# Attention scores from two float32r parts in 64-row groups, in place of three bfloat16 parts in 72 rows

## What is computed

```python
q = split_heads(x @ Wq.T)          # 16 heads of 8, 4 sequences
k = split_heads(x @ Wk.T)
v = split_heads(x @ Wv.T)
q = _rope(q, pos); k = _rope(k, pos)
score = jnp.einsum('bqd,bkd->bqk', q, k)
score = jnp.where(causal[None], score, -jnp.inf)
attn = jax.nn.softmax(score / jnp.sqrt(jnp.float32(D_K)), axis=-1)
out = jnp.einsum('bqk,bkd->bqd', attn, v)
```

## Time and profile before

| what | us |
|---|---|
| median of 3 executions | 916.42 (909.37 to 917.06) |
| span of the profiled execution, first to last instruction | 855.6 |
| from the first tile of attention to the start of the second feed-forward layer | 202.3 to 717.9 |
| one steady stage of attention | 30.31 |

### The profile page before, as it was taken

How to read it: one execution, slowest core, us unless ns; L and a number is a source line. 1 busy time by engine, 2 the same in 40 slices (tenths; PEclk the granted TensorE clock), 3 DMA queues, 4 the chain that set the end, 5 groups by cost and what they waited for, 6 DMA issues and landing times. The chain is left out here.

```text
span 855.6 us, 17846 instructions
## 1 busy us (share of the span) xinstructions
PE 779.7 (91%) x5570; PEld 427.9 (50%) x5570; DVE 610.9 (71%) x1919; ACT 507.4 (59%) x1229; POOL 315.4 (37%) x603
## 2 busy tenths in 40 slices
PE   9889999887899999999999999999999997689995
PEld 8888896543233333333333333333333335579884
DVE  4657774698668777788878878788787722856663
ACT  2166651673247767667667766766777684146662
POOL 6177742475104223223322422331242231056753
PEclk8699999998569999999999999999999998789998
DMA  8721113065332033033113303312320001122110
GB/s 271 270 57 50 54 33 117 23 169 159 57 57 45 14 57 57 10 49 58 34 26 57 53 6 57 58 22 36 57 41 18 3 1 34 73 70 50 52 42 26
DMA packets 27989, 51.84 MB, mean 61 GB/s; under 512 B 7552, under 2 KB 19200, under 8 KB 26496
## 3 DMA queue, kind: packets, MB, share of 16 engines
q1 hardware_dynamic: 21296, 41.04, 20.7%
q0 software_dynamic: 4096, 8.69, 3.8%
q10 hardware_dynamic: 2512, 1.06, 0.5%
HBM read 35.40 MB, written 14.97 MB: 59 GB/s over the span
## 5 line engine op out<-in xcount | busy, mean ns | idle before, releaser
L1448 DVE CUSTOM_DVE_ANT_0 cst<-psS,mask_row 128x768 bf16<-128x768 f32 (+7 forms) x512 | 364.7, 756 | 100.2 <-PE psS L1308 97.6
L1412 ACT ACTIVATE prob<-psST 128x512 f32<-128x512 f32 (+3 forms) x750 | 317.3, 495 | 158.9 <-PE psST L1339 155.2
L1353 PE MATMUL a_psO<-prob,vs 128*32 128x512 f32 (+3 forms) x1536 | 166.7, 506 | 2.8 <-ACT prob L1412 1.7
L1532 POOL TENSOR_TENSOR a_gate<-a_zeros 1x1 f32<-1x1 f32 x128 | 23.7, 185 | 333.7 <-ACT prob L1412 333.7
L1339 PE MATMUL psST<-a_qs,ks 75*128 75x512 bf16 (+1 forms) x480 | 123.7, 327 | 5.9 <-ACT prob L1412 3.5
L1308 PE MATMUL psS<-ks,a_qs 72*128 72x512 bf16 (+2 forms) x480 | 119.0, 337 | 5.6 <-DVE a_rowmax L1448 5.5
L777 POOL DMA_INDIRECT tok<-rows,f_there_number x64 | 61.8, 966 | 86.0 <-DVE f_number L489 42.0
L1308 PEld LDWEIGHTS psS<-ks,a_qs 72*128 72x128 bf16 x480 | 35.6, 99 | 101.1 <-DVE a_rowmax L1448 33.0
L1308 PE MATMUL psS<-ks,qs 72*128 72x512 bf16 (+3 forms) x288 | 75.8, 354 | 6.7 <-DVE a_rowmax L1448 6.5
L1533 POOL TENSOR_SCALAR_AFFINE_SELECT prob<-prob 128x512 f32<-128x512 f32 x128 | 80.3, 627 | 0.0
L1339 PE MATMUL psST<-qs,ks 75*128 75x512 bf16 (+3 forms) x270 | 73.4, 346 | 2.7 <-ACT prob L1412 1.7
(11 more groups left out here) (183 smaller groups left out, 1066.1 us busy)
## 6 DMA issues: line engine op xcount, KB each, us to landing
a_qs<-q_split SPq DMA_DIRECT2D x60, 96.0 KB
rows<-tok SPq DMA_DIRECT2D x8, 536.0 KB, 4.9
ks<-k_split SPq DMA_DIRECT2D x32, 128.0 KB
qs<-q_split SPq DMA_DIRECT2D x36, 96.0 KB
q_split<-p_part SPq DMA_DIRECT2D x24, 128.0 KB, 2.4
k_split<-p_part SPq DMA_DIRECT2D x24, 128.0 KB, 2.4
ks<-k_split SPq DMA_DIRECT2D x16, 192.0 KB
tok<-x_after_first SPq DMA_DIRECT2D x4, 536.0 KB, 5.4
```

Source lines behind the costliest of these rows:

```text
L1353: last = nc.tensor.matmul(psO[32 * h:32 * h + 32, c0:c0 + w], vs[r][:, j, h, :], prob[:, u % RING, h, 0:w], start=(j == 0), stop=(u + 1 in ...
L1412: nc.scalar.activation(prob[:, u % RING, h, 0:w], score_buffer(s, u * QH + h)[:, 0:w], ACT.Exp, scale=SCALE).then_inc(exp_done, 1)
L1448: last = nc.vector.tensor_tensor_reduce(out=out[:, a * CH:a * CH + width], in0=ps[:, a * CH:a * CH + width], in1=mask_row[:, S - width:], ...
```

## The change

q and k are rounded into two float32r parts of 12 bits each (float32r is a 4-byte format of the matrix engine with a shortened mantissa), so a stack has 4 x 8 = 32 rows, and one row of zeros makes it 33 (`PR`); with two rows of maxima a score has 35 rows. Heads 0 and 2 of a stage lie in partitions 0 to 34 of the stack, heads 1 and 3 in partitions 64 to 98, so that neighbouring heads' matmuls use different groups of 64 rows of the array. A late tile is now two heads with one half of the keys: first 512 keys of both, reduced by one plain maximum into `early_max`, then the 128 to 512 others of both, by the custom instruction of before, which starts from `early_max`. The middle parts go from the projection. The tile costs, by which `plan` spreads the tiles, follow the new widths. The maxima are written by four transfers each half, where there was one.

```diff
-KINDS = 3
-PR = KINDS * KINDS * DK
+KINDS = 2
+PR = KINDS * KINDS * DK + 1
+SIDES = 2
+SIDE = P // SIDES
+SH = QH // SIDES
...
-        link(nc.gpsimd.memset(n.ks[r][64:PR + MR, :], 1.0))
+        for a in range(SIDES):
+            link(nc.gpsimd.memset(n.ks[r][a * SIDE + PR - 1:a * SIDE + PR + MR, :].bitcast(F32), 1.0))
...
-STACK_DMAS = 2 * KINDS - 1 + KINDS * NCH
+STACK_DMAS = SIDES * (2 * KINDS + 1)
...
         def subtract_hi(g, k):
-            for i in range(2):
-                dve.wait_ge(hi_done[i], g + 1)
-                wait(dve, lo_done[i], g - 1)
-                nc.vector.tensor_tensor(rest[i][k], rot[i][k], part[i][k][:, 0, :],
-                                        ALU.subtract).then_inc(rest_done[i], 1)
-
-        def subtract_mid(g, k):
-
-            dve.wait_ge(mid_done[0], g + 1)
-            nc.vector.tensor_tensor(part[0][k][:, 2, :], rest[0][k], part[0][k][:, 1, :],
+            dve.wait_ge(hi_done[0], g + 1)
+            nc.vector.tensor_tensor(part[0][k][:, 1, :], rot[0][k], part[0][k][:, 0, :].bitcast(F32),
                                     ALU.subtract).then_inc(lo_done[0], 1)
...
-        def mid(g, k):
-
-            for i in range(2):
-                act.wait_ge(rest_done[i], g + 1)
-                nc.scalar.activation(part[i][k][:, 1, :], rest[i][k], ACT.Copy).then_inc(mid_done[i], 1)
...
-    tiles += [((h,), i) for i in (CB, TB - 1, CB + 1, TB - 2) for h in range(QH)]
+    tiles += [((h, h + 1), i, c0) for i in (CB, TB - 1, CB + 1, TB - 2) for c0 in (0, CH) for h in range(0, QH, 2)]
...
-    tile_cost = [len(heads) * (i + 1) * P + 350 for heads, i in tiles]
+    tile_cost = [len(tiles[t][0]) * tile_width(t) + 350 for t in range(MT)]
...
+    def side(h, rows):
+
+        return slice(h % SIDES * SIDE, h % SIDES * SIDE + rows)
...
-            sp.dma_start(max_rows(r, half), maxT[half][:, :]).then_inc(max_loaded[half], 16)
+            for k in range(QH):
+                a, g = k // SH, k % SH
+                sp.dma_start(max_rows(r, half, g * SIDES + a),
+                             maxT[half][k * MR * CB:(k + 1) * MR * CB, :].bitcast(F32)).then_inc(max_loaded[half], 16)
...
-                lhs = qs[r][0:PR, q_col(h, i * P):q_col(h, i * P) + P]
-                for c0 in range(0, width, CH):
-                    w = min(CH, width - c0)
-                    last = nc.tensor.matmul(ps[:, a * CH + c0:a * CH + c0 + w], lhs,
-                                            ks[r][0:PR, h * S + c0:h * S + c0 + w], start=True, stop=True)
+                last = nc.tensor.matmul(ps[:, a * CH:a * CH + w], qs[r][side(h, PR), q_col(h, i * P):q_col(h, i * P) + P],
+                                        ks[r][side(h, PR), q_col(h, c0):q_col(h, c0) + w], start=True, stop=True)
...
-            nc.tensor.matmul(score_buffer(s, m)[:, 0:w], ks[r][:, h * S + j * P:h * S + (j + 1) * P],
-                             qs[r][:, q_col(h, q0):q_col(h, q0) + w], start=True, stop=True).then_inc(scored, 1)
+            nc.tensor.matmul(score_buffer(s, m)[:, 0:w], ks[r][side(h, PR + MR), q_col(h, j * P):q_col(h, j * P) + P],
+                             qs[r][side(h, PR + MR), q_col(h, q0):q_col(h, q0) + w],
+                             start=True, stop=True).then_inc(scored, 1)
...
+            g = heads[0] // SIDES
+            if i >= CB and c0 == 0:
+                nc.vector.tensor_reduce(early_max[:, :, g, i - CB], ps[:, :].rearrange("p (a w) -> p a w", a=SIDES),
+                                        AX.X, ALU.max).then_inc(use_read, 1)
+                return
             for a, h in enumerate(heads):
+                known = early_max[:, a, g, i - CB:i - CB + 1] if c0 else LOWEST
                 last = nc.vector.tensor_tensor_reduce(
...
         pool.wait_ge(cleared, 1)
+        pool.wait_ge(n.lo_done[1], NC8)
+        clear = Chain(pool, rows_cleared)
+        for r in range(1, RING):
+            for a in range(SIDES):
+                clear(nc.gpsimd.memset(qs[r][zero_row(a), :].bitcast(F32), 0.0))
```

More of the change, by code:

```diff
@@ L9 @@
 BF16 = mybir.dt.bfloat16
+F32R = mybir.dt.float32r
 U32 = mybir.dt.uint32
@@ L802, in ffn, with heads, rows @@
         return rows_written
-STACK_DMAS = 2 * KINDS - 1 + KINDS * NCH
+STACK_DMAS = SIDES * (2 * KINDS + 1)
 PART_ROWS = KINDS * DK
 def stack_parts(n, s, q, k):
[L812 to L820, removed]
+    def heads(source, first, last, a):
+        return source[first * DK:last * DK, ds(s * QH, QH), :].rearrange("d (g a) t -> a d g t", a=SIDES)[a]
+    def rows(stack, a, at, count):
+        here = a * SIDE + at * DK
+        return stack[here:here + count * DK, :].bitcast(F32).rearrange("d (g t) -> d g t", g=SH)
+    for a in range(SIDES):
+        yield rows(k, a, 0, KINDS), heads(n.k_dram, 0, KINDS, a)
+        for c in range(KINDS):
+            yield rows(k, a, KINDS + c, 1), heads(n.k_dram, KINDS - 1 - c, KINDS - c, a)
+        for c in range(KINDS):
+            yield rows(q, a, c * KINDS, KINDS), heads(n.q_dram, 0, KINDS, a)
 def load_stacks(sp, n, s, q, k, loaded):
@@ L863, in project @@
     n.outT = anT[0]
-    rot, tmp, rest = ([[n.prob[:, m, 2 * i + k, :] for k in range(2)] for i in range(2)] for m in range(3))
-    part = [[sb(f"part{i}{k}", [P, KINDS, CH], BF16) for k in range(2)] for i in range(2)]
+    rot, tmp = ([[n.prob[:, m, 2 * i + k, :] for k in range(2)] for i in range(2)] for m in range(2))
+    free = n.shared[:, NT // 2:, :].rearrange("p (i a) d -> p i (a d)", i=2).bitcast(F32R)
+    part = [[sb(f"part{i}", [P, KINDS, CH], F32R), free[:, i, :].rearrange("p (m t) -> p m t", m=KINDS)] for i in range(2)]
     psA, psV = n.psST[0], n.psST[1:3]
@@ L1030, in _ @@
             hi(g, g % 2)
-        mid(NC8 - 1, 1)
     @block.gpsimd
@@ L1040, in subtract_hi @@
         def subtract_hi(g, k):
[L1041 to L1051, removed]
+            pool.wait_ge(hi_done[1], g + 1)
+            nc.gpsimd.tensor_tensor(part[1][k][:, 1, :], rot[1][k], part[1][k][:, 0, :].bitcast(F32),
+                                    ALU.subtract).then_inc(lo_done[1], 1)
         nc.gpsimd.memset(n.mask_row[:, 0:S - P], 0.0).then_inc(n.mask_made, 1)
@@ L1057, in _ @@
             if g >= 1:
[L1058 to L1062, removed]
+                subtract_hi(g - 1, (g - 1) % 2)
+        subtract_hi(NC8 - 1, (NC8 - 1) % 2)
     @block.sync
@@ L1076, in keep @@
                     rows = slice(m * DK, (m + 1) * DK)
[L1077 to L1081, removed]
+                    there = (n.q_dram, n.k_dram)[i][rows, heads, k * CH:(k + 1) * CH]
+                    sp.dma_start(there.rearrange("d h t -> h d t"), part[i][k][:, m, :].bitcast(F32)).then_inc(split_stored[i][k], 16)
         for g in range(EARLY):
@@ L1217, in sem @@
         return ctx.enter_context(nc.semaphore(f"a_{name}"))
-    qs = n.qs + [sb(f"qs{i}", [PR + MR, QH * S], BF16) for i in range(1, RING)]
+    qs = n.qs + [sb(f"qs{i}", [P, SH * S], F32R) for i in range(1, RING)]
     ks, vs = n.ks, n.vs
@@ L1297, in tile @@
         def tile(r, turn, t, index, ps):
-            heads, i = tiles[t]
+            heads, i, c0 = tiles[t]
             if t == 0:
@@ L1502, in split @@
             wait(pool, maxT_ready, 2 * s + half)
-            src = rowmax[:, :, half * CB:(half + 1) * CB]
-            done = order * 4
+            src = rowmax[:, :, :, half * CB:(half + 1) * CB]
+            done = order * 2
             def link(ins, k):
```

88 lines of the change are left out of this document (45 added, 43 removed).

## The result

The changed kernel takes 1170.47 us (median of 4, 1150.02 to 1185.62), the kernel before 916.35 (median of 4). The ratio is 1.264, with a 95% interval of 1.253 to 1.276; it goes by the two shorter runs of the changed kernel, since the other two, the profiled one among them, lie more than 1.5% above the shortest. The forecast was 873. Attention now runs at half of TensorE's clock.

The account below looks back on a forecast made before the run. PE was taken to bound the kernel, with DVE a sixth below it in a fixed order. Stages -31, projection -5 and opening -7 made -43 us: span 812.6 plus 60.8 around it gave 873 us, range 850 to 900.

Parts of the forecast that it names:

- What bounds the kernel: Steady attention stage of 30.31 us: PE first, busy for 28.9 us, DVE (VectorE) next at 24.2, in a fixed order.
- the rival on the clock: Attention: the clock falls to 1.2 GHz, a stage streams 45.8 us; four such stages make 944 us; chance 0.08.
- Tiles in pairs, -3.9 us of PE: Attention tiles: two matmuls in different row groups run together, saving PE 3.9 us a stage.
- first rival: Attention: waits go altogether and scores of neighbouring heads overlap too; a stage of 26.5 us, 846 us; chance 0.08.
- What of it reaches the stage: Attention stage: 27.8 us from the pairs, 28.1 with the transfer wait; fourteen stages give -31 us.
- the sum over units: Twelve units of a stage, each at its largest engine's work: 27.7 us before, 26.5 in the changed kernel.
- the surplus: Real stage 2.6 us over its sum, mainly tiles late behind a weighing; halved to 1.3, range 0 to 2.6.
- The format: Attention scores: float32r costs as bfloat16; weight loads may double but stay hidden, 0.1 us a stage (0 to 0.8).
- The row of maxima, 0.3 us: Attention, SP: four transfers of a half instead of one delay a score, 0.3 us a stage (0 to 1.5).
- VectorE's 24.8 us: Attention stage: eight more instructions add 0.6 us (0 to 1.3), so DVE needs 24.8 us.
- Projection, -5 us: Projection before attention: less DVE subtraction, six groups gain 0.8 us each, -5 us (0 to -7).
- Opening, -7 us: From the first tile to stage 0's turn, mostly at half clock: paired tiles save 7 us (0 to 13).

Follow-up runs that it names:

- e2: The kernel before, with tiles and scores contracting only the first 36 of their 72 and 75 rows; 1218.18 us in one run.
- e1: The changed kernel with each side of a stack filled to 64 rows by zeros in q and ones in k; 965.15 us, ratio 1.047.
- e6: The changed kernel with sides of 64 rows and bfloat16 in place of float32r for q, k and the maxima; 914.59 us in one run.
- e11: e6 with the row of maxima of a half carried by two transfers instead of four, q's columns laid out for it; 899.25 us in one run.
- e9: e6 with a needless VectorE copy of 64 columns out of PSUM ahead of each late tile's maximum; 950.13 us in one run.
- e10: e6 with one needless PE matmul of 512 columns ahead of each late tile; 931.71 us in one run.
- e4: The kernel before with its stacks filled up to 128 rows by zeros in q and ones in k; 914.60 us, ratio 0.997.
- e3: The changed kernel with 160 matmuls over all 128 rows ahead of the first tile in stages 3 and 9; 1184.50 us in one run.
- e8: e4 with its two late fills moved after the first split on GpSimd and half as many numbers; 909.05 us, ratio 0.993.

## Why the prediction was wrong, point by point

- **What bounds the kernel** was read rightly: PE first, VectorE close behind, a fixed order between them.
- **The failed step** is in the rival on the clock: "once slowed PE is full, which ended the slow stretch at 250". The forecast took busy time as what keeps the clock. e2 shows a full PE at 0.50 with nothing changed but the rows, and e1 gives most of the clock back by rows alone. The row that the forecast took for the fall, 205 to 210 us, lies behind it: a mean of 0.56 leaves 0.6 us at the full clock. The change takes each matmul from 72 and 75 rows to 33 and 35. The rival was right in its kind and its price (45.8 us a stage forecast, 48.9 measured); it counted four such stages where all fifteen behind the opening are slow, and had a chance of 0.08.
- **Tiles in pairs, -3.9 us of PE:** the pairs run together, as taken, and PE's busy time of a stage goes from 28.89 to 25.03 in e6, 3.86 less. That the two numbers agree is partly chance: scores of neighbouring heads overlap as well (515.73 above), which the forecast had only in its first rival.
- **What of it reaches the stage:** mis-sized. The forecast had 30.3 fall to 27.8, by the sum over units and half of the surplus. In the old format it falls to 29.9 and 30.6 in turn, 30.24 on average, so the surplus over the 26.5 is 3.7 us, not 1.3. e11 names 0.8 of it, the transfer; how the rest is made up stays open, but e9 and e10 show that work on either engine lengthens it. Halving the surplus rested on a tile that comes late behind a weighing and would come sooner; that was assumed, not read from a row, and the faster tiles didn't bring it.
- **The format:** one pass, as taken. The weight loads were put at 0.1 us of a stage (0 to 0.8), since they stay hidden behind 0.22 us of streaming. The format costs 2.4 us. The load did take double, as said there; the step left out that a score or tile which has waited starts with its load, so that the longer load shows each time. That this makes up the 2.4 us is argued, not counted. With the rows filled and the full clock a stage takes 32.6 us on average (e1), 2.3 more than before: even with the clock a stage loses.
- **The row of maxima, 0.3 us:** right in place, too small; four transfers cost 0.5 us more than two in the short stage and 0.8 on average (e11), with a wait of 1.26 us in the trace of e6.
- **VectorE's 24.8 us:** 25.65 in e1. A custom instruction that takes the earlier maximum costs about 0.06 us more (748 against 689 ns for 512 columns), and a stage has 16 of them; the trace of before couldn't show that.
- **Projection, -5 us:** right. From the products of its second group to the first tile it takes 226.56 - 185.67 = 40.9 us, 45.7 in the profile of before.
- **Opening, -7 us:** 1.2 measured (277.54 - 226.56 = 51.0 us from the first tile to the turn, 52.1 before), both at half clock for most of it; nearer to VectorE's end of the range (0) than to PE's (-13).

The chances were wrong as well: 0.17 for slower, where two mechanisms pointed there: the clock by itself, and by the stage of e1 (2.3 us more, fourteen times) the format too.

## What to carry to other kernels

Before matmuls are made narrower in rows, or moved into row groups, look at the granted clock of stretches with few rows, not only at PE's busy share: half the rows can cost half the clock (e2), and rows of zeros and ones bought most of it back (e1), at no cost in a steady stage of the kernel before (30.30 us in e4, 30.31 without). When an engine's work is shortened in a fixed order between two engines of equal load, expect a small part of it in the time (here 0.1 of 3.9 us on average, 0.9 with the two transfers of e11), and price the longer weight loads and extra transfers against that part, not against the whole. Test it with a little needless work on each engine: the one whose work shows in full is the bound. Here neither did (1.2 of 1.9 us, 1.2 of 1.5 us, one run each).

## What the runs showed of the hardware that was not expected

- TensorE's granted clock went with the rows that matmuls use: 36 rows of 128, 0.50 with PE busy for 99.5% of a stage, but for three stretches of 17 us (e2); 72 and 75 rows, 1.00 at 95%; 62 and 64 rows in float32r, the tiles in pairs, 1.00 in some stages and down to 0.71 in others (e1). Rows that multiply zeros by ones counted. With 62 and 64 rows something else counted too: e9 keeps e6's matmuls, has PE idle for longer, and falls to 0.85 in 9 of 14 stages.
- A burst of 160 full matmuls lifted it, and it was at 0.50 again within 4 us of the burst's end (e3).
- float32r streams 512 columns in 0.23 us at the full clock (729.78 to 730.01 in e1), bfloat16 in 0.22. Its weight loads take 185 ns at the full clock and 0.30 to 0.32 us on average at half (changed kernel; 0.29 for two that run together, 515.14), those of bfloat16 94 to 97 ns and 0.12 to 0.15 us (e2).
- Matmuls of neighbouring heads, in the two groups of 64 rows, start together: two tiles (515.14) and two scores (515.73) of the changed kernel, and the same in e1 (729.78).
- Which feature of the rows counts (cells switched on, operands read, weights held) wasn't separated. Nor is it known why the usual executions spend about 60 us more around attention than the profiled one of before; the mean clock differs there (0.84 in e8 against 0.94 in the first 185 us, 0.85 against 0.91 behind the last turn), which may be cause or effect.
